# Attention on one Trainium2 core: where the first iteration copies its second value tile, and where the second heads of a pair are scaled

## What is computed

```
qkv    = einsum('bsh,ph->bsp', layernorm(x), weight_qkv)     # 4 groups of 4 q heads, one k and one v, 128 wide
scores = einsum('bsgqd,btgd->bgqst', q, k) / sqrt(128)
attn   = softmax(where(causal, scores, min))
x      = x + einsum('bse,he->bsh', einsum('bgqst,btgd->bsgqd', attn, v), weight_proj)
```

## Time and profile before

| | us |
|---|---|
| median of 3 runs | 602.51 |
| lowest, highest of the 3 | 600.58, 925.73 |
| profiled execution | 605.44 |
| its span (first to last instruction) | 603.6 |
| PE busy | 578.8 (96%) |
| DVE busy | 489.1 (81%) |
| ACT busy | 371.0 (61%) |
| POOL busy | 231.4 (38%) |

### The profile page before, as it was taken

How to read it: one execution, slowest core, us unless ns; L and a number is a source line. 1 busy time by engine, 2 the same in 40 slices (tenths; PEclk the granted TensorE clock), 3 DMA queues, 4 the chain that set the end, 5 groups by cost and what they waited for, 6 DMA issues and landing times.

```text
span 603.6 us, 13020 instructions
## 1 busy us (share of the span) xinstructions
PE 578.8 (96%) x4180; PEld 543.5 (90%) x4180; DVE 489.1 (81%) x1527; ACT 371.0 (61%) x1039; POOL 231.4 (38%) x326
## 2 busy tenths in 40 slices
PE   8799999999999999999999999999997987899996
PEld 7699999999999999999999999999986977788885
DVE  4889889878978987896898789878875986768876
ACT  5786657556655665576576656668874755444553
POOL 4566224233323422332342234233547785402120
PEclk9999999999999999999999999999997998989999
DMA  8702400000000000000000000000000000000012
GB/s 325 268 2 74 146 2 2 1 1 0 0 0 0 0 0 0 0 0 0 0 0 0 0 0 0 0 1 2 1 2 0 2 2 0 4 1 18 18 35 71
DMA packets 9121, 14.73 MB, mean 24 GB/s; under 512 B 1536, under 2 KB 6656, under 8 KB 9088
## 3 DMA queue, kind: packets, MB, share of 16 engines
q1 hardware_dynamic: 9088, 14.30, 6.8%
HBM read 12.20 MB, written 2.10 MB: 24 GB/s over the span
## 4 chain that ended last, share of the span: by engine, by line
PE 76%; DVE 11%; ACT 4%; issue 3%; POOL 3%; DMA 0%; DVEq 0%; POOLq 0%; ACTq 0%
PE bank L610 63%; PE bank L673 4%; PE bank L687 4%; PE bank L690 2%; PE bank L620 2%; ACT prob L1060 2%; DVE pT L1369 2%; DVE prob L1435 1%; PE bank L785 1%; DVE prob L1414 1%; ACT qT L1023 1%; DVE ternary_stats L1558 1%; DVE prob L1623 1%; PE bank L854 1%; POOL qkv L455 1%
## 5 line engine op out<-in xcount | busy, mean ns | idle before, releaser
L499 POOL TENSOR_SCALAR prob<-prob,rowinv 128x128 f32<-128x128 f32 (+1 forms) x128 | 106.7, 843 | 270.9 <-DVE rowinv L1432 270.9
L610 PE MATMUL bank<-xT,big 128*128 128x256 f32 x1008 | 133.5, 285 | 0.4 <-DVE xT L1369 0.4
L610 PEld LDWEIGHTS bank<-xT,big 128*128 128x128 f32 x1008 | 127.4, 193 | 1.4 <-issue 0.6
L1060 ACT ACTIVATE prob<-prob,negmax 128x128 f32<-128x128 f32 (+1 forms) x256 | 112.9, 444 | 19.4 <-DVE negmax L1426 19.3
L610 PE MATMUL bank<-wp,oT 128*128 128x256 f32 x768 | 102.3, 283 | 0.0
L610 PEld LDWEIGHTS bank<-wp,oT 128*128 128x128 f32 x768 | 96.8, 190 | 0.7
L1023 ACT ACTIVATE qT<-bank 128x512 fp32r<-128x512 f32 x68 | 40.6, 597 | 71.6 <-PE bank L610 71.6
L610 PE MATMUL bank<-pT,v 128*128 128x512 f32 (+1 forms) x384 | 80.3, 344 | 3.9 <-DVE v L1369 2.4
L610 PEld LDWEIGHTS bank<-pT,v 128*128 128x128 f32 x384 | 63.1, 189 | 14.9 <-DVE v L1369 2.8
L1369 DVE TENSOR_TENSOR pT<-bank,pT 128x512 fp32r<-128x512 f32 (+1 forms) x128 | 64.8, 547 | 2.1 <-ACT pT L1023 2.1
L1369 DVE TENSOR_TENSOR qT<-bank,qT 128x512 fp32r<-128x512 f32 x68 | 46.8, 689 | 19.5 <-ACT qT L1023 19.0
(11 more groups left out here) (161 smaller groups left out, 1025.9 us busy)
## 6 DMA issues: line engine op xcount, KB each, us to landing
x<-in_x SPq DMA_DIRECT2D x8, 256.0 KB, 7.2
raw<-in_wq SPq DMA_DIRECT2D x4, 512.0 KB, 8.5
raw<-in_wp SPq DMA_DIRECT2D x4, 512.0 KB, 8.1
out<-x SPq DMA_DIRECT2D x8, 256.0 KB, 2.1
raw<-in_w_gu SPq DMA_DIRECT2D x2, 640.0 KB, 4.6
raw<-in_w_in SPq DMA_DIRECT2D x1, 768.0 KB, 4.8
raw<-in_w_down SPq DMA_DIRECT2D x1, 640.0 KB, 6.3
raw<-in_wk SPq DMA_DIRECT2D x1, 512.0 KB, 3.6
```

Source lines behind the costliest of these rows:

```text
L499: m = pool.tensor_scalar(prob[:, j % 2, 0, a:b], prob[:, j % 2, 0, a:b], rowinv[:, j % 2, r:r + 1], None, ALU.mult)
L610: m = pe.matmul(out, lhs(a), rhs(b), start=first and i == 0, stop=last and i == len(passes) - 1, skip_group_check=True)
L1060: m = act.activation(prob[:, j % 2, i, a:b], prob[:, j % 2, i, a:b], ACT.Exp, scale=SCALE, bias=negmax[:, 2 * i + r:2 * i + r + 1], accum_ ...
```

## The change

Two things. In element 0, iteration 0, ACT takes `v_hi(0, 1)` and `q_hi(0, 3)` ahead of the late weight and of `Abs`, and DVE takes `v_lo(0, 1)` and `q_lo(0, 3)` ahead of `row_max(0, 2)`. And in all elements DVE's `normalise` is split: `invert_sums(j+2)` (the reciprocals) stays where `normalise` was, and the two multiplications of pair `j+2` follow one iteration later, behind the next `row_max`. No instruction is added or removed; PE's, POOL's and SP's orders are as they were.

```
@@ ACT, batch @@
                 for j in range(J):
                     pT_hi(n, j)
+                    first = isinstance(n, int) and n == 0 and j == 0
+                    if first:
+                        v_hi(n, 1)
+                        q_hi(n, 3)
...
-                    if j == 0:
+                    if j == 0 and not first:
                         v_hi(n, 1)
                     if j in (5, 6) and not last:
                         k_hi(n + 1, j - 5)
-                    if j < J - 3 or not last:
+                    if not first and (j < J - 3 or not last):
                         q_hi(*ahead(n, j, 3))
@@ DVE @@
-            def normalise(n, j):
+            def invert_sums(n, j):
                 t = J * n + j
                 dve.wait_ge(s_ex, t + 1)
                 dve.reciprocal(rowinv[:, j % 2, :], rowsum[:, :]).then_inc(s_ri, 1)
-                dve.wait_ge(s_ri, t + 1)
+
+            def normalise(n, j):
+
+                dve.wait_ge(s_ri, J * n + j + 1)
                 for r, (a, b) in enumerate(((0, P), (P, 3 * P))):
@@ DVE, batch @@
                     pT_lo(n, j, 1)
+                    first = isinstance(n, int) and n == 0 and j == 0
+                    if first:
+                        v_lo(n, 1)
+                        q_lo(n, 3)
                     if j < J - 2 or not last:
                         row_max(*ahead(n, j, 2))
-                    if j == 0:
+                        if not first:
+                            normalise(*ahead(n, j, 1))
+                    if j == 0 and not first:
                         v_lo(n, 1)
...
-                    if j < J - 3 or not last:
+                    if not first and (j < J - 3 or not last):
                         q_lo(*ahead(n, j, 3))
...
                         if j == 6:
+                            invert_sums(n, J - 1)
                             normalise(n, J - 1)
...
                     if j < J - 3 or not last:
-                        normalise(*ahead(n, j, 2))
+                        invert_sums(*ahead(n, j, 2))
```

## The result

The changed kernel took 598.7 us (median), the kernel before beside it 602.27; the ratio is 0.995, with a 95% interval from 0.992 to 0.997. The forecast was 602.0 with a range of 598.5 to 605.5: the change lies within 2%, the time inside the range, 0.2 us above its lower end. The forecast gain was 0.5 us, the medians differ by 3.6. One run of the changed kernel took 794.8 us at a mean clock of 0.655, and one of the kernel before 925.73; the medians include them, the ratio does not. The two questions are where the gain comes from, and how much of it is the change.

What follows compares the result with a forecast made beforehand. PE's own work was taken to bound the loop; in element 0, a chain through POOL's normalise, late_lo and negmax. +1.6 in element 0 and -2.1 in the loop gave -0.5 from the 602.51 median: 602.0 us, range 598.5 to 605.5.

Steps and rivals of the forecast that it cites:

- The wait of 2.36 us: Element 0, iteration 0: PE's idle for v_lo before attend(0)'s second half goes, but most is given back within one iteration.
- the two places named: scores(3) and attend(1) in element 0, where an idle of PE of about 1 us was to stand instead.
- The rival that pays in full: Element 0: negmax only slow beside POOL, so the 2.36 us stay gained; 597.4 us in all, chance 0.2.
- negmax is held by POOL: Element 0, iterations 1 to 3: DVE's negmax ends 0.03 us behind POOL's late_lo, which holds it until over.
- The head's +1.6 us: Element 0: delays through iterations 0 to 3 make scores(6) start at 51.4 instead of 49.77, costing 1.6 us.
- The rival of the freer POOL: Element 0: without multiplications beside it POOL's normalise is 0.23 us shorter three times; cost +0.9, total 601.3, chance 0.15.
- The sign I had named for it: POOL's normalise shorter than 1.69 us would show that POOL runs freer.
- PE, then full, keeps this shift: After iteration 3 of element 0, without late_lo, PE was to keep the whole 1.6 us delay.
- The loop's -2.1 us: Iteration 1 of elements 1 to 6 and the last: o_lo starts 0.3 us earlier, PE gains 0.3 each time.
- The rival in which the loop gives nothing: Loop: another wait behind pT_lo's, for instance scores for q_lo, takes the 0.3 us; total 604.1, chance 0.15.
- the slow one: Loop: multiplications ahead of q_lo make PE wait at scores, 30 iterations at 0.47, 14 us; some 618 us, chance 0.05.
- The lower bound: Loop gain: at least what PE's recorded waits for pT_lo add up to, 0.9 us in all.

Runs made afterwards that it cites:

- e: The kernel before with POOL's late_lo(4) to late_lo(7) cut to 16 of 1024 columns, the rest zeroed early; 601.68 us, one run.
- f: The changed kernel with POOL's late_lo(4) to late_lo(7) cut to 16 of 1024 columns, the rest zeroed early; 599.98 us, one run.
- c: The changed kernel with the multiplications split off only from element 1 on; 599.80 us, ratio 0.995 to the kernel before.
- d: As c, but with DVE's q_lo(0, 3) back behind row_max(0, 2); 598.13 us, ratio 0.993 to the kernel before.
- k: As d, with each of POOL's late_lo(3) to late_lo(7) in four pieces; 604.20 us, one run.
- a: The changed kernel with the split undone, leaving only the new order of the first iteration; 601.01 us, ratio 0.997 to the kernel before.
- b: The changed kernel with the first iteration back in its old order, leaving only the split; 599.05 us, ratio 0.995 to the kernel before.
- h: As d, with each of POOL's late_lo(4) to late_lo(7) in four pieces of 256 columns; 598.73 us, ratio 0.994 to the kernel before.
- l: As k, but with DVE's old order in the first iteration, row_max(0, 2) ahead of v_lo and q_lo; 598.29 us, ratio 0.994 to the kernel before.
- g: The changed kernel with each of POOL's late_lo(4) to late_lo(7) in four pieces of 256 columns; 602.59 us, one run.
- the padding: The changed kernel with 16 extra PE transposes, about 1.9 us, ahead of the last element; 601.27 us, ratio 0.999 to the kernel before.

## Why the prediction was right, and where it was not

**The wait of 2.36 us moves, it is not removed: right.** Iteration 0 became 2.48 us shorter and the next 2.54 longer, with 1.03 and 1.05 us of idle at the two places named. The changed trace begins its first `p_transpose` at 21.28 and before's at 21.78, so 0.50 must be added to compare starts: reciprocals at 31.62 (forecast 31.6), negmax ending at 29.68 (29.7). The rival that pays in full had negmax only slow and not held; e refutes that, and in f, without POOL's hold, the two iterations are no shorter either.

**negmax is held by POOL: right.** In iteration 3 it ends at 49.19, POOL's instruction at 49.16; e shows the cause by taking the instruction away.

**The head's +1.6 us: wrong in size, +0.6 measured.** Step by step, with the 0.50 added:

- Reciprocals of iteration 0: forecast +0.5, measured 31.62 - 31.07 = +0.55.
- POOL's `normalise`: I took no change. It takes 1.50 us now and 1.65 before (the row below). The multiplications beside it make the difference: c, d and k, which have them there in element 0, take 1.65 too.

```profile
31.35 1.65 POOL L499 TENSOR_SCALAR prob<-prob,rowinv 128x128 f32<-128x128 f32 x2 [2.24 <-DVE rowinv L1432]
```

  Three times 0.15 come off the chain: `late_lo` of iteration 2 starts +0.26, and its negmax ends +0.27 instead of +0.5. The rival of the freer POOL was in part right, with 0.15 each where it put 0.23. The sign I had named for it, less than 1.69 us, was none: in element 0 it was 1.65 already before.
- Reciprocals of iteration 2: forecast +1.0, measured 44.54 - 43.81 = +0.73, which is 0.26 and the 0.47 of the multiplications.
- negmax of iteration 3: forecast +1.1, measured 49.69 - 49.12 = +0.57.
- `scores(6)`: forecast +1.6, measured 50.79 - 49.77 = +1.02.
- "PE, then full, keeps this shift" failed. From `scores(6)` to `attend(4)` PE took 53.27 - 49.77 = 3.50 us before, with a wait of 0.17 for `pT_lo`, and 53.38 - 50.29 = 3.09 now (c, with the multiplications in their old place: 53.32 - 49.82 = 3.50). The multiplications are gone from ahead of `pT_lo` there as well. I had counted this gain in the loop and not in element 0; it is 0.41 us, and leaves +0.60.

In the sum: 0.55 - 0.45 + 0.47 + 0.47 - 0.41 = 0.63, where the two 0.47 are the multiplications ahead of `q_lo` in iterations 2 and 3. The forecast was above it by the 0.45 of POOL, which I had left out, the 0.41 of `pT_lo`, and some 0.1 of rounding up.

The runs split the +0.6 otherwise than I did: a has +0.53 from the new order alone, b +0.07 from the split alone. The split's costs and gains in element 0 cancel.

**The loop's -2.1 us: right.** An element takes 0.30 us less six times (324.48 to 322.67), and the last stretch 0.45 instead of 0.3: together -2.26. The waits for `pT_lo` are gone, none for `q_lo` has come. The rival in which the loop gives nothing and the slow one both fell. The lower bound that the prediction took from the waits, 0.9 us in all, was less than half of what came.

**The time.** With the two right sizes the sum is -1.7, not -0.5, and the median would have been put at 600.8. The measured 598.7 lies lower by the clock, which I had allowed for only as a spread: the 602.51 of before stood 2.2 us above its time at a clock of 0.990, and the runs of the changed kernel lie near that clock. That the time falls inside the range is owed to that allowance, with 0.2 us to spare, and so is in part luck; the sum foretold 0.5 us of gain where attention alone gave 1.7.

## What to carry to other kernels

A wait of the bounding engine is worth only what lies between it and the next wait on the same chain: follow the chain one iteration further before counting it. A split that frees a late instruction in the loop was worth more than a wait eight times as long as its own at the head, since it comes seven times. The waits on record (0.9 us) were less than half of what it freed. And where VectorE's small instructions stand beside long GpSimd ones, look at how long the same small instruction takes elsewhere: in element 0 no new order won anything in five iterations, and cutting the long instruction into pieces won 1.5 us.

## What the hardware showed that I had not expected

**Pieces of 256 columns let VectorE in, memsets did not.** A negmax beside four pieces takes at most 0.48 us in h, and 0.75 and 0.76 in l and g. In e, POOL's four zero fills, which only write, held VectorE's layer norm for all of their time, 3.86 us for what takes 0.73 otherwise, and PE with it:

```profile
5.55 0.94 POOL L551 MEMSET wp<- 128x1008 f32 x1
5.72 3.86 DVE L1368 TENSOR_SCALAR xn<-x,moments,rstd 128x256 f32<-128x256 f32 x2 [1.23 <-POOL rstd L433]
6.42 0.94 POOL L551 MEMSET big<- 128x1008 f32 x1
7.30 1.82 POOL L551 MEMSET wp<- 128x1008 f32 x2
...
9.64 1.11 PE L625 MATMUL bank<-ident,xn 128*128 128x128 f32 x4 [3.86 <-DVE xn L1368]
```

The rows show both, not why the one lets VectorE in and the other doesn't. The Trainium skill ("SBUF — State Buffer", "Who interferes with whom") says that a `tensor_scalar` of VectorE in a two-port mode and a GpSimd instruction exclude each other for the whole of the one that began first. By that rule VectorE should have got in behind the first memset, at 5.55 + 0.94 = 6.49; the row, which holds two instructions, ends only at 9.58, 0.46 us behind the last memset, and one of the two alone took 3.55 us, where most of this line take 0.4. The hold agrees with the rule; that it outlasts four instructions does not follow from it.

**GpSimd pays too, but little.** Its scaling of a first head takes 1.64 to 1.68 us beside the two multiplications and 1.50 to 1.52 without them.

**The granted clock goes with 0.5 us for each 0.001 of its mean.** How low it is differs between runs of one kernel, by more than the change is worth, and neither the runs nor the padding settle what decides it.
